# Second norm of an attention block: scale and offset applied to its tile instead of folded into the MLP's weights and bias

## What is computed

```
xn = layernorm(x)
# branch 1, on xn: a linear-attention block that ends with an MLP
x = ... attention, output projection, depthwise convolution ...
xn2 = (x - mean(x)) * rsqrt(var(x) + eps) * norm2_g + norm2_b      # over the 256 channels
mlp = gelu(xn2 @ fc1_w + fc1_b) @ fc2_w + fc2_b                    # 256 -> 1024 -> 256
branch1 = x + mlp
# branch 2, on xn: gated feed-forward with ternary weights
h = silu(xn @ w1.T * w1_s) * (xn @ w2.T * w2_s)                     # 256 -> 1024
h = gelu(h @ h1.T * h1_s); h = gelu(h @ h2.T * h2_s)                # 1024 -> 1024, twice
branch2 = h @ w3.T * w3_s
out = x + branch1 + branch2
```

## Time and profile before

| | before |
|---|---|
| runs, us | 1064.75, 1066.06, 1067.23 |
| median, us | 1066.06 |
| span of the profiled execution, us | 1062.1 |
| TensorE busy | 1025.0 us, 96% |
| VectorE busy | 759.1 us, 71% |
| ScalarE busy | 603.4 us, 57% |
| GpSimd busy | 236.0 us, 22% |
| granted TensorE clock, mean over the span | 0.996 |

### The profile page before, as it was taken

The page is one execution under the profiler, slowest core; times in us unless marked ns, Lnnn a source line. Parts: engine busy times, 40 slices in busy tenths (PEclk is TensorE's granted clock), DMA queues, the critical chain, the costliest instruction groups (busy, mean ns, idle before and its releaser), DMA issues. The chain is left out here.

```text
span 1062.1 us, 17208 instructions
## 1 busy us (share of the span) xinstructions
PE 1025.0 (96%) x6644; PEld 908.3 (86%) x6644; DVE 759.1 (71%) x962; ACT 603.4 (57%) x875; POOL 236.0 (22%) x214
## 2 busy tenths in 40 slices
PE   3999999999999999999999999999999999999998
PEld 3778777888777777887788889989899999999998
DVE  6874688535548578888877556867878968776664
ACT  4788667675444374565555525556656654665444
POOL 3453255234306111111110130231200211101100
PEclk9999999999998999999999999999999999999999
DMA  8989614956884635524312574233494423222310
GB/s 317 398 263 377 195 67 154 328 202 199 296 279 153 206 121 179 179 81 148 110 61 80 197 268 133 81 116 127 153 375 160 159 81 120 90 73 81 115 41 22
DMA packets 68258, 180.15 MB, mean 170 GB/s; under 512 B 5024, under 2 KB 26144, under 8 KB 64544
## 3 DMA queue, kind: packets, MB, share of 16 engines
q1 hardware_dynamic: 68176, 179.03, 48.7%
HBM read 121.34 MB, written 66.06 MB: 176 GB/s over the span
## 5 line engine op out<-in xcount | busy, mean ns | idle before, releaser
L2272 PE MATMUL pr<-xp_hi,wb 128*128 128x256 f32 x1344 | 320.2, 282 | 0.9 <-DVE u L2006 0.7
L2272 PE MATMUL pr<-xp_lo,wb 128*128 128x256 f32 x1344 | 319.7, 281 | 0.0
L2272 PEld LDWEIGHTS pr<-xp_hi,wb 128*128 128x128 f32 x1344 | 255.2, 190 | 2.7 <-issue 2.6
L2272 PEld LDWEIGHTS pr<-xp_lo,wb 128*128 128x128 f32 x1344 | 255.8, 190 | 0.0
L2272 PE MATMUL pr<-u_hi,ring 128*128 128x512 f32 x256 | 102.4, 400 | 1.8 <-POOL u_lo L934 1.0
L2272 PE MATMUL pr<-u_lo,ring 128*128 128x512 f32 x256 | 100.0, 391 | 0.0
L1423 ACT CAST xp_hi<-tf 128x1024 fp32r<-128x1024 f32 x48 | 50.2, 1046 | 56.6 <-PE pr L2272 19.9
L1053 POOL TENSOR_TENSOR ot<-ot,yg 128x512 f32<-128x512 f32 x14 | 25.2, 1801 | 244.4 <-DVE ot L2051 244.4
L1859 DVE TENSOR_TENSOR h_lo<-hf,h_hi 128x512 fp32r<-128x512 f32 x64 | 54.8, 863 | 32.5 <-ACT h_hi L1363 32.5
L2457 PE MATMUL pr<-wf_hi,h_hi 128*128 128x256 f32 x256 | 75.3, 294 | 0.6 <-DVE h_lo L1859 0.6
L2000 DVE TENSOR_TENSOR xp_lo<-tf,xp_hi 128x1024 fp32r<-128x1024 f32 x48 | 60.8, 1267 | 20.2 <-ACT xp_hi L1423 20.1
(11 more groups left out here) (237 smaller groups left out, 2522.7 us busy)
## 6 DMA issues: line engine op xcount, KB each, us to landing
ring<-w_s SPq DMA_DIRECT2D x42, 512.0 KB, 7.4
uf<-h_s SPq DMA_DIRECT2D x16, 1024.0 KB, 5.0
wb<-s_s SPq DMA_DIRECT2D x8, 1024.0 KB, 9.1
wb<-w_s SPq DMA_DIRECT2D x6, 1024.0 KB, 10.5
vw<-v_s SPq DMA_DIRECT2D x8, 514.0 KB, 6.6
xt<-x SPq DMA_DIRECT2D x8, 512.0 KB, 6.1
xn_s<-xh SPq DMA_DIRECT2D x8, 512.0 KB, 8.9
stage<-w_gated SPq DMA_DIRECT2D x2, 2048.0 KB, 12.8
```

The costliest lines, as they stand in the source:

```text
L2272: return e.matmul(bank, w.bitcast(dt), v_.bitcast(dt), start=first, stop=last, skip_group_check=True)
```

## The change

The scale and offset of the second norm move from the weights and the bias to the tile. ScalarE now reads the tile in PSUM four times: for each of its two chunks it writes `x * norm2_g + norm2_b` rounded into `pm_hi`, and for each of them once more unrounded into `pm`, which lies where `pm_lo` lies. VectorE subtracts `pm_hi` from `pm`, both in SBUF, and writes `pm_lo` over `pm`. `fc1_w` is split as it is, by one copy and one subtraction over both chunks. The products with `norm2_b`, the addition that made `fb`, the tile `fb` and the waits for them go; the GELU takes `fc1_b` itself. `norm2_tokens` waits for ScalarE's writes (`m_hi`) instead of VectorE's (`m_lo`), since only ScalarE reads `Y`.

```diff
@@ high_of_fc1 (ScalarE)
-                for k in range(KC):
-                    last = e.activation(wf1_hi[:, k, :], wf1_raw[:, k, :], ACT.Copy, scale=par("norm2_g", k))
-                last.then_inc(s["w_set"], 1)
+                e.copy(wf1_hi[:], wf1_raw[:]).then_inc(s["w_set"], 1)
@@ high_of_norm2 (ScalarE)
-                e.copy(pm_hi[:], Y[:]).then_inc(s["m_hi"], 1)
+                for out_ in (pm_hi, pm):
+                    for k in range(KC):
+                        last = affine(out_[:, k, :], Y[:, k, :], par("norm2_g", k), par("norm2_b", k))
+                last.then_inc(s["m_hi"], 1)
@@ gelu (ScalarE)
-                    e.wait_ge(s["biased"], 2)
-                    last = e.activation(out_, F1[:, m % 2, :], ACT.Gelu, bias=fb[:, m:m + 1])
+                    last = e.activation(out_, F1[:, m % 2, :], ACT.Gelu, bias=par("fc1_b", m))
@@ low_of_mlp_weights, mlp_offsets, low_of_norm2 (VectorE)
-                for k in range(KC):
-                    last = e.scalar_tensor_tensor(out=wf1_lo[:, k, :], in0=wf1_raw[:, k, :], scalar=par("norm2_g", k),
-                                                  in1=wf1_hi[:, k, :].bitcast(F32), op0=ALU.mult, op1=ALU.subtract)
-                last.then_inc(s["w_lo"], 1)
-            def mlp_offsets():
-                e.wait_ge(s["offsets"], 2)
-                e.tensor_tensor(fb[:], kv_bank[:, 0:KH], prm[:, at_:at_ + KH], ALU.add).then_inc(s["biased"], 1)
+                e.tensor_tensor(wf1_lo[:], wf1_raw[:], wf1_hi[:].bitcast(F32), ALU.subtract).then_inc(s["w_lo"], 1)
-                e.tensor_tensor(pm_lo[:], Y[:], pm_hi[:].bitcast(F32), ALU.subtract).then_inc(s["m_lo"], 1)
+                e.tensor_tensor(pm_lo[:], pm[:], pm_hi[:].bitcast(F32), ALU.subtract) \
@@ offsets_of_mlp, norm2_tokens, fc1, fc2 (TensorE)
-            def offsets_of_mlp():
-                e.wait_ge(s["wf_in"], 48)
-                e.wait_ge(s["e_masked"], BATCHES)
-                for m in range(KH):
-                    for k in range(KC):
-                        last = e.matmul(kv_bank[:, m:m + 1], wf1_raw[:, k, m * P:(m + 1) * P], par("norm2_b", k),
-                                        start=(k == 0), stop=(k == KC - 1))
-                last.then_inc(s["offsets"], 1)
-                e.wait_ge(s["m_lo"], i)
+                e.wait_ge(s["m_hi"], i)
-                    e.wait_ge(s["biased"], 2)
@@ SyncE, ahead of the residual loads
-                    sp.wait_ge(s["offsets"], 2)
```

More of the change, by code:

```diff
@@ L280, in program @@
         w1p, w2p = keep("w1p", [P, KC]), keep("w2p", [P, KC])
-        ab, fb = keep("ab", [P, 2 * KC]), keep("fb", [P, KH])
+        ab = keep("ab", [P, 2 * KC])
         small = keep("small", [P, 2, SUB])
@@ L358, in program @@
         pm_hi, pm_lo = (place(n, [P, KC, TOK], RD + 57472 + 4096 * i, F32R) for i, n in enumerate(("pm_hi", "pm_lo")))
+        pm = place("pm", [P, KC, TOK], RD + 57472 + 4096)
         h_hi, h_lo = (place(n, [P, KH, TOK], RG + 16384 * i, F32R) for i, n in enumerate(("h_hi", "h_lo")))
@@ L1785, in low_of_mlp_weights @@
                 e.wait_ge(s["w_set"], 4)
-                for k in range(KC):
-                    last = e.scalar_tensor_tensor(out=wf1_lo[:, k, :], in0=wf1_raw[:, k, :], scalar=par("norm2_g", k),
-                                                  in1=wf1_hi[:, k, :].bitcast(F32), op0=ALU.mult, op1=ALU.subtract)
-                last.then_inc(s["w_lo"], 1)
-            def mlp_offsets():
-                e.wait_ge(s["offsets"], 2)
-                at_ = PARAMS["fc1_b"][0]
-                e.tensor_tensor(fb[:], kv_bank[:, 0:KH], prm[:, at_:at_ + KH], ALU.add).then_inc(s["biased"], 1)
+                e.tensor_tensor(wf1_lo[:], wf1_raw[:], wf1_hi[:].bitcast(F32), ALU.subtract).then_inc(s["w_lo"], 1)
             def denominators(b):
@@ L1852, in low_of_norm2 @@
                 e.wait_ge(s["m_hi"], i + 1)
-                e.tensor_tensor(pm_lo[:], Y[:], pm_hi[:].bitcast(F32), ALU.subtract).then_inc(s["m_lo"], 1)
+                e.tensor_tensor(pm_lo[:], pm[:], pm_hi[:].bitcast(F32), ALU.subtract) \
+                    .then_inc(s["m_lo"], 1)
             def low_of_gelu(i, m):
@@ L1954, in _ @@
                 front("e", i, "after_num2")
-                if i == E_STEPS[1]:
-                    mlp_offsets()
                 if valid(i + 3):
@@ L2477, in second_half @@
                         spread_z(i + 3)
-                    if i == E_STEPS[1]:
-                        offsets_of_mlp()
                     front(wide, "e", i, "after_z")
```

## The result

The changed kernel takes 1073.34 us (median of four runs, 1071.53 to 1073.85). The kernel before took 1066.64 us beside it (four runs, 1064.75 to 1067.33). The ratio is 1.006, with an interval of 1.0048 to 1.0073. That is 6.7 us more (1073.34 less 1066.64), where 4.4 were predicted, and the median lies 0.7 us over the top of the range (1072.6).

A forecast was written before the change was run, and what follows sets the result against it. TensorE, busy 1025 of 1062.1 us, was taken to bound the kernel. 0.78 (H0) + 1.65 (tile 0) + 0.69 (tile 6) + 1.30 (tile 7) = 4.4 us, added to 1066.06, gave 1070.5 us, range 1066.0 to 1072.6.

The forecast's parts named there:

- Removed products: Ahead of H0: removing 16 offset products gains nothing, since VectorE gates G6 at 342.48 us whatever TensorE did before.
- Eight slow products: In H0, behind TensorE's gap: eight products at 0.43 instead of 0.23 us, making its fifteenth product 0.78 us later.
- The path behind H0: From H0 to tile 0's norm: no term of its own; from 330 us on TensorE was said to hardly wait.
- H0's term: At H0's fifteenth product: 0.78 us later, carried into the sum; 0.57 us earlier if the clock holds, 1.6 later with twelve.
- Tile 0's wait: Before tile 0's first fc1 product: all the added ScalarE time reaches TensorE, 1.65 us (1.46 to 1.95).
- Tiles 6 and 7: Before these tiles' fc1: delays of 0.69 us (0.50 to 0.99) and 1.30 us (1.11 to 1.60).
- The four activations: ScalarE, the norm's tile: a pace of 0.59 to 0.71 us each, 1.65 us more per tile than the cast.
- The 4.0 us carried from the span to the median: Whole kernel: the median lies 4.0 us over the profiled span, so the 4.4 us were added to 1066.06.
- The clock did not hold: Rival, gap ahead of H0: clock holds, +3.1 us in all, 1069.1 us; chance 0.15.
- VectorE did not come sooner by more than 0.14 us: Rival, G6's gating: VectorE gets there 1.1 us sooner and the clock holds, +2.0 us, 1068.1 us; chance 0.13.
- the whole 6.8 us: Rival, offset products: all their TensorE time comes out, -3.2 us in all, 1062.9 us; chance 0.08.
- The rival of both high ends: Rival, H0 and the norm's tile: twelve slow products and the 0.71 us pace, 1072.2 us; chance 0.15.

The follow-up runs named there:

- GELU first: Changed kernel with the last hidden unit's GELU on ScalarE moved right behind the four activations, ahead of the convolution taps: 1070.06 us, ratio 1.0033.
- halves: Changed kernel with the norm's activations ordered chunk by chunk, a signal behind each, and VectorE's subtraction in two halves: 1071.76 us, ratio 1.0058.
- the norm alone: Changed kernel with the 16 offset products put back at their old place, their result unused: 1069.96 us, ratio 1.0036.
- the filled gap: Changed kernel with 24 unread products of 512 columns put ahead of H0, where TensorE waits: 1072.22 us, ratio 1.0051.
- the gating first: Changed kernel with VectorE gating G6 and G7 ahead of the four taps and making the MLP weights' low parts later: 1066.14 us, ratio 1.0002.
- the last move: First tile's norm put ahead of its residual on GpSimd and VectorE, added to the changed kernel with four earlier moves (1063.92 us): 1060.50 us, ratio 0.9951.
- the kernel before with the moves: Kernel before, offset products kept, with early gating on VectorE, GpSimd's wf2_lo subtraction late, first tile's norm ahead of its residual: 1064.76 us, ratio 0.9988.

## Why the prediction was wrong

The direction and the places of the predicted waits were right. Three steps were not: the count of slow products behind the gap, the path from H0 to tile 0's norm, which had no term, and the price of tile 0's wait, which had none for slow products.

- **Removed products.** The step that found them worth nothing holds: G6's gating was expected at 342.38 us in the old trace's time, and came at 343.26 with an offset of 0.92; H0 was expected at 342.45 and came at 343.37. The 0.1 us saved by `wf1_lo` was 0.14. Removing them alone cost 1.6 us.
- **Eight slow products: the first step that failed.** The prediction took eight from a stretch of twelve and one of four, and twelve as the high end. Behind the same gap of 5.8 to 6.0 us the profiled executions show 14 (the changed kernel), 6 (products removed), 12 (GELU first) and 11 (halves). The count is no property of the gap alone, and twelve was not its end. H0's fifteenth product was expected at 347.27 us and came at 349.42, which is 348.50 in the old trace's time: 1.2 us more. The Trainium skill (TensorE: Matmul & The Clock Gate, What's actually happening) says that one kernel's count of slow products at its start was 6, 11 or 14 from run to run, and warns against fitting to one. The counts here are no test of that, being of four kernels in mid-kernel, one execution each; they spread as widely, 6 to 14.
- **The path behind H0: the second step that failed.** The sum carried H0's delay to tile 0 one to one, and "it hardly waits" passed over TensorE's wait of 0.77 us for `xnt` in the trace of before. Where H0's fifteenth product was late by just the predicted 0.78 us (the products removed), TensorE left that wait 1.6 us late, because the residual's transfer landed 1.6 us late. And with 11, 12 and 14 slow products it left the wait at the same time within 0.1 us, 378.6 us in the old trace's time, having waited 1.32, 1.21 and 0.92 us there. So of the 1.4 us that H0's term lacks, some 0.8 belong to this path and 0.6 to the count; this split is an estimate from these four executions.
- **Tile 0's wait: the third step that failed.** The 1.65 us was right (1.76). But the step put the clock's fall on the 6.4 us gap alone, and counted a wait of 1.9 us at its length. In three of the five profiled executions that have this wait (the change, the norm alone, the halves) nine slow products follow; in two (the filled gap, the gating first) none do. The missing term is 1.3 us where it comes, and in the run with the GELU first neither the wait nor the slow products are left.
- **Tiles 6 and 7.** 0.69 and 1.30 us against 0.8 and 1.4. Tiles 1 to 5 at nothing, as said: VectorE's `pm_lo` of tile 1 lay between other work.
- **The four activations.** A pace of 0.66 us, between the ends of 0.59 and 0.71.
- **The 4.0 us carried from the span to the median.** Every run of the experiments stands 1.7 to 1.9 us over its own span, so the other 2.2 say only that the profiled execution of before took 2.2 us less than the median. It did no harm, since the difference was added to the median.
- **The rivals.** The clock did not hold, VectorE did not come sooner by more than 0.14 us, and the whole 6.8 us did not come out. The rival of both high ends, 1072.2 us, was the nearest; with the missing term of 1.3 us it gives 1073.5, which is near the measured 1073.34 partly by luck: it has two slow products too few, and a slower pace of the activations than measured.

## What to carry to other kernels

Before counting removed work as a gain, run the consumer's other operand forward: here VectorE's order held H0 at the same time, and removing 4.4 us of TensorE's work alone cost 1.6 us, until one move on VectorE released it. Price a new wait of TensorE at its length plus the slow products behind it, with a range as wide as the counts seen (here 0 to 9 behind 1.9 us, 6 to 14 behind 6 us). Carry a delay forward only as far as TensorE's next wait, and work out that wait again: here it took up the difference between 11 and 14 slow products. When a stall is gone, look for the next in the same trace: the last move, worth 3.4 us, was on a norm that had waited 0.8 us before.

## What the runs showed of the hardware

- The clock can fall behind a wait of 1.9 us, and not at once: in the changed kernel five products ran at 0.23 us after the wait, and then nine at up to 0.43 us. With the same wait it held in other executions. What decides between them is not settled. The three executions with the stretch are also the three in which the clock had fallen between 331 and 350 us; no run tells whether that matters. Behind the wait of 2.76 us it fell too (eight slow products). Behind the waits of 0.39, 0.91 and 1.54 us shown above it stayed at 1.00.
- The clock fell while 32 passes of one column ran back to back, with TensorE busy throughout: in the kernel before it is 1.00 in 331.0 to 333.0 us, 0.64 in 333.0 to 335.4 us and 0.50 behind the earlier trace rows. It fell there again in the kernel before with the moves (0.51).
- VectorE's instruction on 128x4 took 2.33 us beside a GpSimd addition of 2.38 us, and 0.17 us without one. So here an instruction of four numbers a partition took as long as its neighbour's 1024.
